# A two-layer graph network: 23 of 25 chunks of the last stage issued inside the second layer's loop

## The reference, cut to what matters

```
h        = relu(layernorm(x))
dinv     = rsqrt(deg)
features = segment_sum((h @ W_gcn)[src] * dinv[src] * dinv[dst], dst)      # 12500 nodes
update   = relu(features @ W1 + b1) @ W2 + b2
out      = x + update
```

## Time and profile before

| what | us |
|---|---|
| median of 3 runs (lowest, highest) | 6323.46 (6308.38, 6337.69) |
| the profiled execution's own time | 6340.04 |
| its span, first to last instruction | 6337.5 |
| loop of the second layer's stage, first to last eviction | 4739.67 to 6268.36 |
| last stage | 6277.05 to 6337.5 |

### The profile page before, as it was taken

How to read it: one execution, slowest core, us unless ns; L and a number is a source line. 1 busy time by engine, 2 the same in 40 slices (tenths; PEclk the granted TensorE clock), 3 DMA queues, 4 the chain that set the end, 5 groups by cost and what they waited for, 6 DMA issues and landing times. The chain is left out here.

```text
span 6337.5 us, 128256 instructions
## 1 busy us (share of the span) xinstructions
PE 5203.0 (82%) x34818; PEld 3460.6 (55%) x34818; DVE 4202.3 (66%) x13257; ACT 4829.9 (76%) x11024; POOL 3254.9 (51%) x3411
## 2 busy tenths in 40 slices
PE   6755548888788888888788888787669999999998
PEld 5411115555455555555555555554437777777777
DVE  5577775555555555555555555555449999999996
ACT  3566647778777777777777777777339999999996
POOL 3577757777777777777777777777310000000000
PEclk7555557777876687776877667778559999999998
DMA  4444433433433333343333333433111111111121
GB/s 155 139 124 123 123 87 94 113 93 96 114 94 113 93 94 111 93 112 91 94 112 94 108 96 93 114 94 96 55 53 63 63 63 73 74 63 63 63 77 71
DMA packets 329554, 593.56 MB, mean 94 GB/s; under 512 B 142708, under 2 KB 199044, under 8 KB 316692
## 3 DMA queue, kind: packets, MB, share of 16 engines
q1 hardware_dynamic: 216868, 329.75, 16.5%
q0 software_dynamic: 103344, 158.83, 11.6%
q10 hardware_dynamic: 8640, 96.77, 4.0%
HBM read 430.51 MB, written 154.44 MB: 92 GB/s over the span
## 5 line engine op out<-in xcount | busy, mean ns | idle before, releaser
L978 POOL DMA_INDIRECT gbuf<-a_tab,idxb x2688 | 2596.4, 966 | 927.2 <-issue 793.6
L1888 ACT ACTIVATE nf<-psum 128x600 bf16<-128x600 f32 x2604 | 1522.4, 760 | 12.2 <-PE psum L1879 5.4
L1078 DVE TENSOR_TENSOR pre<-psum,gbuf 128x384 f32<-128x384 f32 x806 | 449.6, 558 | 1395.6 <-PE psum L1065 1192.2
L1065 PE MATMUL psum<-rhs,lhs 128*128 128x96 f32 x6448 | 1192.1, 345 | 0.1
L1879 PE MATMUL psum<-x_all 128*128 128x300 bf16 x5208 | 1071.7, 292 | 76.5 <-DVE x_all L1872 31.6
L1065 PEld LDWEIGHTS psum<-rhs,lhs 128*128 128x128 f32 x6448 | 1066.4, 250 | 106.2 <-issue 60.2
L1871 DVE TENSOR_SCALAR x_all<-x_all,dstrel 128x600 bf16<-128x600 f16 x2604 | 966.3, 371 | 100.6 <-PE psum L1879 11.0
L1109 PE MATMUL psum<-msg,oh 128*128 128x388 f32 x1612 | 981.5, 703 | 0.0
L1119 ACT ACTIVATE x_all<-psum 32x97 f32<-32x97 f32 x3224 | 782.5, 243 | 132.7 <-PE psum L1129 93.4
L1197 ACT ACTIVATE x_all<-psum 128x300 bf16<-128x300 f32 x1260 | 524.3, 416 | 386.4 <-PE psum L1186 385.1
L1901 PE MATMUL psum<-x_all,nf 128*128 128x96 bf16 x12400 | 805.1, 205 | 1.2 <-issue 0.6
(11 more groups left out here) (231 smaller groups left out, 6332.0 us busy)
## 6 DMA issues: line engine op xcount, KB each, us to landing
adj_tab<-x_all ACTq DMA_DIRECT2D x60, 1575.0 KB
gbuf<-a_tab,idxb POOLq DMA_INDIRECT x3224
x_all<-dst_row SPq DMA_DIRECT2D x806, 64.0 KB
x_all<-adj_tab SPq DMA_DIRECT2D x30, 1575.0 KB, 6.5
x_all<-attr_parts SPq DMA_DIRECT2D x807, 36.0 KB
x_all<-attr_parts SPq DMA_DIRECT2D x403, 72.0 KB
spilled<-gbuf SPq DMA_DIRECT2D x134, 192.0 KB, 1.9
gbuf<-spilled SPq DMA_DIRECT2D x134, 192.0 KB
```

What stands on the lines that cost most here:

```text
L978: g.indirect_dma_start(gbuf[:, k % 4, t, :], None, a_tab[:, :], bass.IndirectOffsetOnAxis(ap=idxb[:, k % 4, t:t + 1], axis=0)).then_inc(g_ ...
L1065: ins = pe.matmul(ps_m(k)[:, t, :], lhs[:, k % 2, t * TILE:(t + 1) * TILE], rhs[:, k % 2, :], start=True, stop=True)
L1888: act.activation(adj[:, w % 2, :, j * SLOT:(j + 1) * SLOT].rearrange("p (b h) s -> p b h s", b=2), ps_a(n).rearrange("p b (h s) -> p b h s ...
```

## The change

Each of 23 chunks is finished inside the second layer's loop, as soon as the groups that can touch it have been added to `sT`. Which loop that is follows from a bound: group g must begin no earlier than node 81 g - 160 (`pace`, `LAG`). The bound is tested on the device in the first stage: a row of 154 values (`paced`) is made on GpSimd, VectorE subtracts the groups' first nodes and takes the maximum, and the result joins the six flags that were there. With the numbers of this problem, `ready` names 23 pairs of (q, chunk): q from 2 to 30 without 4, 9, 13, 18, 23 and 28, and chunks 0 to 22.

For such a q, in loop w = 4q + 1: ScalarE issues one relu behind the eviction of tile j = 9, TensorE one fp32 matmul behind the sums of each of the tiles j = 11, 12, 13 and 14 (into bank 7, which is free then), VectorE four outputs behind the one-hots of j = 17. SP loads the chunk's rows of x behind the load of the early table and stores the result. Only chunks 23 and 24 are left for the last stage, whose code becomes a function, `last_stage(tag, first, count)`; the general pass calls it for the other 23. Cut to its core:

```diff
+LAG = 160
+        self.pace = n * GT * TILE // e
+        self.ready = {}
+        for q in range(1, self.ND // 4):
+            done = self.pace * self.late[4 * q] - LAG
+            if CH * (len(self.ready) + 1) <= done:
+                self.ready[q] = len(self.ready)
+        self.HID = len(self.ready)
...
+                dve.wait_ge(gb_ok, 2)
+                link(dve.tensor_tensor(paced[:, :], paced[:, :], gt_f[0:1, 0:NG], ALU.subtract))
+                dve.tensor_reduce(flag_f[0:1, 6:7], paced[:, :], AX, ALU.max).then_inc(viol_ok, 1)
...
+        def now_rows(sp, q):
+            c = d.ready[q]
+            if c:
+                sp.wait_ge(o_now, 16 * c)
+            sp.dma_start(acc[:, :, :], resid[:, cols(c), :]).then_inc(l_now, 16)
+        def now_store(sp, q):
+            c = d.ready[q]
+            sp.wait_ge(n_out2, c + 1)
+            sp.dma_start(out[:, cols(c), :], acc[:, :, :]).then_inc(o_now, 16)
+        def now_relu(act, q):
+            c = d.ready[q]
+            act.wait_ge(w_add, 4 * q)
+            act.wait_ge(hw_add, q)
+            if c:
+                act.wait_ge(n_o, c)
+            act.activation(z_now, sT[0:H + 1, chunk(c)], ACT.Relu).then_inc(n_z, 1)
+        def now_product(pe, q, t):
+            c = d.ready[q]
+            if t == 0:
+                pe.wait_ge(n_z, c + 1)
+            ins = pe.matmul(bank[7][:, t * C:(t + 1) * C], every(z_now, t), w2[:, :], start=True, stop=True)
+            if t == CT - 1:
+                ins.then_inc(n_o, 1)
+        def now_output(dve, q):
+            c = d.ready[q]
+            dve.wait_ge(n_o, c + 1)
+            dve.wait_ge(l_now, 16 * (c + 1))
+            for t in range(CT):
+                n = c * CT + t
+                ins = dve.scalar_tensor_tensor(acc[:, t, :], bank[7][:, t * C:(t + 1) * C], dinv[:, n:n + 1], acc[:, t, :],
+                                               ALU.mult, ALU.add)
+            ins.then_inc(n_out2, 1)
...
+                if e in d.ready:
+                    pe.wait_ge(n_out2, d.ready[e] + 1)
...
-                    for e in range(NE):
-                        early_load(sp, e)
+                    for e in range(ND // 4):
+                        if e < NE:
+                            early_load(sp, e)
+                        if e in d.ready:
+                            now_rows(sp, e)
+                            now_store(sp, e)
+                    sp.wait_ge(o_now, 16 * d.HID)
...
+                            if w % 4 == 1 and w // 4 in d.ready and 11 <= j < 11 + CT:
+                                now_product(pe, w // 4, j - 11)
...
+                        if w % 4 == 1 and w // 4 in d.ready and j == 9:
+                            now_relu(act, w // 4)
...
+                            if w % 4 == 1 and w // 4 in d.ready and j == 17:
+                                now_output(dve, w // 4)
...
         with nc.Else():
             general_pass("_g", False)
+            last_stage("_g", 0, d.HID)
         end_stage()
+        last_stage("", d.HID, NCH - d.HID)
```

More of the change, by code:

```diff
@@ L157, in gnn_kernel @@
         ones = sb("ones", [P, P])
-        flag_f = sb("flag_f", [P, 12])
-        limits = sb("limits", [P, 6])
+        flag_f = sb("flag_f", [P, 14])
+        limits = sb("limits", [P, 7])
+        paced = sb("paced", [1, NG])
         gbase_i = sb("gbase_i", [1, NG], I32)
@@ L321, in _ @@
                        allow_small_or_imprecise_dtypes=True).then_inc(c_pool, 1)
-                g.wait_ge(c_pool, 14)
+                g.iota(paced[:, :], [[d.pace, NG]], base=-LAG, channel_multiplier=0,
+                       allow_small_or_imprecise_dtypes=True).then_inc(c_pool, 1)
+                g.wait_ge(c_pool, 15)
                 g.memset(limits[:, 0:1], float(W - 1)).then_inc(c_pool, 1)
@@ L336, in _ @@
                                     ALU.subtract).then_inc(centred, 1)
-                g.wait_ge(viol_ok, 6)
-                g.partition_all_reduce(flag_f[:, 6:12], flag_f[:, 0:6], P, RMAX).then_inc(viol_all, 1)
+                g.wait_ge(viol_ok, 7)
+                g.partition_all_reduce(flag_f[:, 7:14], flag_f[:, 0:7], P, RMAX).then_inc(viol_all, 1)
             @block.tensor
@@ L416, in _ @@
                 dve.wait_ge(viol_all, 1)
[L417 to L418 removed]
+                link(dve.tensor_tensor(flag_f[:, 7:14], flag_f[:, 7:14], limits[:, :], ALU.is_le))
+                link(dve.tensor_reduce(flag_f[:, 0:1], flag_f[:, 7:14], AX, ALU.min))
                 link(dve.tensor_copy(flag_i[:, :], flag_f[0:1, 0:1]))
@@ L1857, in gnn_kernel @@
         BJ = 7
+        z_now = msg[:, :, :, :].rearrange("p k t c -> p (k t c)")[0:H + 1, 0:CH]
+        n_z = sem("n_z")
+        n_o = sem("n_o")
+        n_out2 = sem("n_out2")
+        l_now = sem("l_now")
+        o_now = sem("o_now")
+        def now_rows(sp, q):
[25 more added lines that the diff above has]
+            dve.wait_ge(l_now, 16 * (c + 1))
+            for t in range(CT):
+                n = c * CT + t
+                ins = dve.scalar_tensor_tensor(acc[:, t, :], bank[7][:, t * C:(t + 1) * C], dinv[:, n:n + 1], acc[:, t, :],
+                                               ALU.mult, ALU.add)
+            ins.then_inc(n_out2, 1)
         def share(n, steps, q):
@@ L2051, in gnn_kernel @@
             general_pass("_g", False)
+            last_stage("_g", 0, d.HID)
         end_stage()
[L2058 to L2063, removed]
-        f_o = signal("f_o", 2)
-        f_out = signal("f_out", 2)
-        f_st = signal("f_st", 2)
-        o_out = [sem("o_out0"), sem("o_out1")]
-        def final_relu(act, i, k):
-            if final.absent(i, k):
-                return
-            c = 2 * i + k
-            act.wait_ge(f_o.sem, f_o.at(c - 2))
-            act.activation(z_sb[:, k, :], sT[0:H + 1, chunk(c)], ACT.Relu).then_inc(f_zr.sem, 1)
@@ L2076, in final_product @@
-        def final_product(pe, i, k):
-            if final.absent(i, k):
-                return
-            c = 2 * i + k
-            pe.wait_ge(f_zr.sem, f_zr.at(c))
-            pe.wait_ge(f_out.sem, f_out.at(c - 2))
-            for t in range(CT):
-                ins = pe.matmul(ps_chunk(4 + k)[:, t, :], every(z_sb[:, k, :], t), w2[:, :], start=True, stop=True)
-            ins.then_inc(f_o.sem, 1)
-        def final_output(dve, i, k):
-            if final.absent(i, k):
-                return
-            c = 2 * i + k
-            if c % RC == 0:
-                dve.wait_ge(l_res[c // RC], 16)
-            dve.wait_ge(f_o.sem, f_o.at(c))
-            dve.wait_ge(f_st.sem, f_st.at(c - 2))
-            for t in range(CT):
-                n = c * CT + t
-                ins = dve.scalar_tensor_tensor(o_sb[:, k, t, :], ps_chunk(4 + k)[:, t, :], dinv[:, n:n + 1],
-                                               x_all[:, n:n + 1, :].rearrange("p t c -> p (t c)"),
-                                               ALU.mult, ALU.add)
-            ins.then_inc(f_out.sem, 1)
```

122 lines of the change are left out of this document (80 added, 42 removed).

## The result

| kernel | median of runs | lowest to highest | runs |
|---|---|---|---|
| before | 6329.03 us | 6308.38 to 6339.79 | 22 |
| with the change | 6344.72 us | 6328.39 to 6370.23 | 22 |

The ratio is 1.0025 [1.0017, 1.0033]: 10.8 to 20.9 us slower, where 13.0 us less was forecast, and above the range that was given. The loss is small, but its sign is sure.

What follows compares the result with a forecast made beforehand. ScalarE, with TensorE and VectorE nearly full, bounds the loop; TensorE's fp32 matmuls bound the last stage. Last stage -51.7, loop +38.2 (1.66 us for each of 23 chunks), first stage +0.5: -13.0, median 6310.5 us, range 6286 to 6332.

Steps and rivals of the forecast that it cites:

- The last stage: Stage after the loop: with two chunks left it lasts 8.7 us instead of 60.45, 51.7 us less.
- The price of a product: TensorE in the loop: one fp32 product alone between bf16 work costs 0.38 us, 1.52 for four; ends 0.25 and 0.50.
- The rule that the forecast set beside it: Weight load time goes by columns at 1.2 GHz, whatever the rows: a lone product 0.52 us, the loop pays 51 us.
- The wait for the relu: Loop 61, before a chunk's first product: TensorE waits 0.45 us for ScalarE's relu, with everything on TensorE queued behind.
- ScalarE's lag: Loop 61: ScalarE runs 0.41 us behind TensorE, so 0.41 comes off each chunk's cost.
- VectorE's 0.10: Four outputs behind tile 17's one-hots: the lead of three tiles just covers them; 0.10 us added a chunk.
- The clock in the loop: TensorE's clock stays at 1.00 in the loop; a fall below would prove the forecast wrong, no row giving a reason.
- The first stage: Two more VectorE operations and a wait ahead of the mean cost 0.5 us, nothing to 1.
- The first: Rival: only ScalarE's share counts in the loop, 0.52 us a chunk, 12.0 for 23; sum -39.2, 6284.4 us; chance 0.13.
- The second: Rival: a lone fp32 product in the loop costs 0.50 us as at half clock; sum -2.0, 6321.5 us; chance 0.14.
- The third: Rival: VectorE's lead is gone, tile 18's one-hots are waited for, 2.55 us a chunk; sum +7.5, 6330.9 us; chance 0.10.
- The fourth: Rival: the seventh flag fails and the general pass runs, a time no row shows; chance 0.01.

## Why the prediction was wrong

- **The last stage**, 8.7 us forecast, 8.57 measured: right, with the walk that led to it. The load of x was hidden, but barely: it was issued at 6327.13, and the first chunk's outputs waited for it until 6330.82; they end at 6331.81, and the second chunk's begin at 6332.07.
- **The price of a product** is the step that failed, the term "I take 0.38", with its ends of 0.25 and 0.50. It is 0.74, 33 us more over 92 products. Twice the wrong row was asked. The lower end and the value came from L1065, whose weights lie side by side. The upper end came from the last stage, read as slow because its clock was half; its loads take 304 to 328 ns there and 304 to 328 ns in the loop at full clock, so the full clock gives it nothing back, and 0.50 was a price in a row, not an upper end. That row alone couldn't tell: side by side, four products in a row at the low clock take 0.50 each too; the loads of the two layouts at full clock could. Two pairs of kernels show the stride: 1.30 against 1.05 us for a slot, with 316 against 184 ns for a load, and 13.44 against 12.45 for a loop. By the runs the 0.74 are 0.28 (back to back with side-by-side weights), 0.25 for the stride, 0.21 for standing alone.
- **The rule that the forecast set beside it** (the Trainium skill, TensorE: Matmul & The Clock Gate, "LDWEIGHTS (loading the stationary operand)") gave an estimated 0.52 for a product alone, and with weights side by side 0.49 was measured: there it was nearer than my 0.38. Its step from 32 to 128 columns, an estimated 80 ns, agrees with the traces: 108 ns a record for `group_place`, 184 for the product. Its 107 ns for 128 columns doesn't agree with the 184. It counts columns and knows no stride.
- **A rule that bears on the stride.** The load that reads every fourth fp32 value takes 316 ns instead of 184, and the relu that does so 1137 instead of 641. The Trainium skill (SBUF — State Buffer, in a note in "Door 1: The DMA port swizzle (why `[64,N]` ≈ `[32,N]`)") says that SBUF, the memory that holds these operands, has lines of 16 bytes and that each access to a new line pays. Four fp32 values are 16 bytes, so here every access goes to a new line; the traces agree in that both get slower. The same note gives four fp32 values as how far one can stride for free; taken as a stride of four, the traces don't agree. No run has another stride, so that the line is the reason is argued, not shown.
- **The wait for the relu**, 0.45 forecast, is 0.21, and it isn't a cost by itself: moving the relu took it away and gained nothing. The walk let the relu begin when the eviction ahead of it had ended; it is done 0.38 us after that end rather than 0.52, for it begins 0.27 us before (5503.44, where two evictions that start at 5502.34 take 1.37 us).
- **ScalarE's lag**, 0.41 forecast, gave back 0.42, as what is left of 3.17: right for this kernel.
- **VectorE's 0.10** is nothing: with one output instead of four the loop is as long. With products at 0.74 it had more time between tables than the walk gave it.
- **What the sum didn't have:** the clock in the loop (8.8 us in the profiled execution), which the forecast named as a way to be wrong, and the gap behind the loop (3.5 us, of which the copy is 3.1), which it took as unchanged, though the diff shows the code growing on the side that isn't taken.
- **The first stage**, 0.5 forecast, reads 0.7.

With the measured terms: -51.9 + 63.3 + 8.8 + 3.5 + 0.7 = +24.4 us, or +23.4 with the 1.0 that the other loops took less. The medians show 10.8 to 20.9, so 2.5 us or more of this are in the profiled execution alone. What the low stretches cost changes between executions: 8.8 us here and 8.7 without the other side's last stage, 5.5 with one output, where the loop issues the same products. That could be the difference; it isn't shown.

**The rivals.** The first (only ScalarE's 0.52) falls: TensorE's work comes through, less the 0.42 of the lag. The second had the right term and, for weights side by side, the right price of 0.50, but not this kernel's. The third had the right sign by a mechanism that isn't there: three outputs fewer change nothing. The fourth didn't come.

**What stays open** is why the clock falls. The forecast saw no reason for it in the rows. It fell in all six traces in which products load with the stride one at a time or in a row of four (five, two, three, three, one and three stretches), in none of the four with weights side by side, and not with a single strided product for each chunk. All 17 falls begin 2.1 to 4.7 us behind a chunk's first product, while its four products run or as they end. So it goes together with the strided products, with one trace for each kernel; no run shows by what in them.

## What to carry to other kernels

Price an instruction by rows with its layout, not only its shape: for fp32 weights, ask how the operand lies in memory, and when an instruction is as long at half the clock as at full, something else bounds it. When work moves into a pipelined loop, the cost is set by the tiles it lands in: four products with weights side by side cost 1.96 us behind tiles that carried sums, and 0.84 behind tiles in which TensorE waited anyway. A stage that is taken away is worth its length less the price at the new place, and small prices come many times: here the stage gave 52 us, and the 92 products alone took 68.

## What the runs showed of the hardware

- A load of 33x128 fp32 weights is two records. At full clock each takes 184 ns side by side and 316 with every fourth value. At half the clock the strided record takes 326 (33 rows), and one side by side, of 128 rows, 333 instead of 192. On ScalarE a relu of 33x512 takes 641 ns, and 1137 when it reads every fourth value.
- One fp32 product of 96 columns costs 0.28 us in a row (128 rows of weights), 0.49 alone between bf16 matmuls (33 rows); with the stride 0.53 and 0.74 (33 rows). In a row at half the clock it costs 0.50 in either layout.
- VectorE's 128x128 bf16 operation of 0.25 us took 1.09 and 0.66 beside a GpSimd operation of 2.05 us. The Trainium skill (SBUF — State Buffer, "🔬 SBUF: two separate sides") says that these two engines share a pair of ports that one holds for a whole instruction. The trace agrees that one waits for the other: 0.84 and 0.41 us were lost. It doesn't show a hold for the whole instruction: VectorE's operation ends at 5517.34, and GpSimd's, whose records are rough, at 5518.17.
- Code on the side of a branch that isn't taken: with a copy of the last stage there the gap behind it was 4.57 us (4.04 to 4.75 in ten traces), without it 1.46.
